# Third node stage of a four-layer graph network: residual and bias summed in PSUM by TensorE instead of in SBUF by VectorE

## The reference

```python
rst = jax.ops.segment_sum(msg, dst, num_segments=N)
rst = rst + bias[None, :, :]
...
x = _layernorm(x + _L2_gnn_ref(x, edge_attr_64, src, dst, ...), axis=-1)
```

## Time and profile before

| | |
|---|---|
| median of three runs | 9195.85 us (9191.78 to 9219.41) |
| profiled execution | 9210.81 us |
| its span | 9209.1 us |
| VectorE busy | 6234.8 us, 68% |
| GpSimd busy | 5451.7 us, 59% |
| TensorE busy | 4799.2 us, 52% |
| ScalarE busy | 3278.4 us, 36% |
| DMA traffic | 1839.84 MB, 200 GB/s |

### The profile page before, as it was taken

One profiled execution on the slowest core, in us unless ns is written; L12 is line 12 of the kernel. 1 busy time (PEld: TensorE's weight loads), 2 busy tenths in 40 slices (PEclk: granted clock), 3 DMA queues, 4 the chain that ended last, 5 costly groups with the idle time before them and its releaser, 6 DMA issues. The chain is left out here.

```text
span 9209.1 us, 103278 instructions
## 1 busy us (share of the span) xinstructions
PE 4799.2 (52%) x18908; PEld 3452.2 (37%) x18908; DVE 6234.8 (68%) x20123; ACT 3278.4 (36%) x8442; POOL 5451.7 (59%) x5121
## 2 busy tenths in 40 slices
PE   8856000039996333347771111100688887899743
PEld 4422000038884211225551111100455555788622
DVE  7899333358887999977777777799544444455566
ACT  4433002347774111126660000144222222344588
POOL 7877777764445666655547777677788888100000
PEclk9999555569997555569995555555777778899855
DMA  0299899989886445459984444588544444566688
GB/s 20 99 344 338 284 309 297 309 274 299 297 294 195 146 146 148 147 173 285 278 268 117 122 122 123 165 266 266 108 79 79 79 79 79 165 200 199 214 292 284
DMA packets 1143019, 1839.84 MB, mean 200 GB/s; under 512 B 218094, under 2 KB 564898, under 8 KB 1142374
## 3 DMA queue, kind: packets, MB, share of 16 engines
q1 hardware_dynamic: 884838, 1245.79, 39.8%
q0 software_dynamic: 257536, 587.44, 26.3%
HBM read 1044.55 MB, written 788.03 MB: 199 GB/s over the span
## 5 line engine op out<-in xcount | busy, mean ns | idle before, releaser
L717 POOL DMA_INDIRECT st<-S,last_i x1176 | 1325.6, 1127 | 897.6 <-DVE yt L759 370.4
L915 POOL DMA_INDIRECT rows<-T,src_i x784 | 800.8, 1021 | 251.1 <-issue 248.1
L642 ACT ACTIVATE xo<-z,shift,rsd 128x256 f32<-128x256 f32 x1568 | 851.0, 591 | 1.3 <-issue 1.1
L1128 POOL DMA_INDIRECT A<-comb,ai x392 | 702.5, 1792 | 159.6 <-issue 145.0
L931 PE MATMUL psE<-encs,attr 4*128 4x256 f32 x784 | 404.9, 668 | 745.2 <-DMA attr<-in_attr3T 745.2
L946 ACT ACTIVATE ex<-diff 128x32 f32<-128x32 f32 x392 | 89.8, 229 | 1709.6 <-DVE diff L993 1709.6
L1200 DVE TENSOR_SCALAR eq<-psI,src_f 128x128 f32<-128x128 f32 x392 | 136.7, 349 | 743.2 <-DMA A<-comb,ai 708.4
L931 PE MATMUL psE<-fes,attr 64*128 64x8 f32 x784 | 199.5, 363 | 821.7 <-DMA attr<-in_attr64T 819.4
L477 DVE SCALAR_TENSOR_TENSOR sums<-sums,same,rows 128x256 f32<-128x256 f32 x784 | 380.2, 485 | 326.6 <-ACT rows L458 312.4
L1142 PE MATMUL psH<-rbf,wf1s 20*128 20x256 f32 x784 | 278.9, 485 | 613.9 <-DMA rbf<-in_rbfT 613.9
L931 PEld LDWEIGHTS psE<-encs,attr 4*128 4x128 f32 x784 | 227.5, 319 | 922.3 <-DMA attr<-in_attr3T 884.7
(11 more groups left out here) (232 smaller groups left out, 15612.8 us busy)
## 6 DMA issues: line engine op xcount, KB each, us to landing
X<-xo SPq DMA_DIRECT2D x588, 256.0 KB
xt<-X SPq DMA_DIRECT2D x588, 256.0 KB
S<-sums SPq DMA_DIRECT2D x392, 272.0 KB, 2.4
A<-zero SPq DMA_DIRECT2D x392, 256.0 KB, 4.8
S<-sums SPq DMA_DIRECT2D x392, 256.0 KB, 4.1
xt<-in_x SPq DMA_DIRECT2D x392, 256.0 KB
T<-tt SPq DMA_DIRECT2D x196, 280.0 KB
T<-tt SPq DMA_DIRECT2D x196, 272.0 KB
```

Source lines behind the costliest of these rows:

```text
L642: ins = e.activation(y[s][:, k, :], z[s][:, k, :], ACT.Identity, bias=shift[s][:, k, :], scale=rsd[s][:, k, :])
L717: e.indirect_dma_start(st[s][:, k, :], None, sums_table, bass.IndirectOffsetOnAxis(ap=last_i[:, c:c + 1], axis=0))\
L915: e.indirect_dma_start(rows[s][:, k, :], None, table, bass.IndirectOffsetOnAxis(ap=src_i[:, c:c + 1], axis=0))\
L1128: e.indirect_dma_start(A[k], bass.IndirectOffsetOnAxis(ap=ai[s][:, k, :], axis=0), comb[s][:, k, :], None, compute_op=ALU.add).then_inc(si ...
```

## The change

`add_bias` is no longer in VectorE's list for `layer` = 2. TensorE gets a part `join_residual` there: for each of the two columns it multiplies the residual by the identity matrix into a PSUM bank and accumulates onto it the product of a row of ones with one row of the bias, so that the bank holds residual plus bias. Two banks `psZ` are used in turn. VectorE's `add` takes its second operand from the bank. A row of 128 ones is set in `setup`.

```diff
+        one_row = sb("one_row", [1, P])
...
+                        e.memset(one_row[:], 1.0)
                         link(e.memset(unit[:], 1.0))
...
-                psZ = [bank(f"psZ{j}", G * D) for j in range(2)] if layer == 0 else None
+                psZ = [bank(f"psZ{j}", G * D) for j in range(2)] if layer != 1 else None
...
                             hold(e, *done(st_["biased"], i, s))
-                            e.tensor_tensor(z[s][:], more, xb[s][:], ALU.add).then_inc(signal(st_["summed"], s), 1)
-
-
-                        unrolled(R, NS, [(combine, 0), (add_bias, 0), (add, ADD), (lambda i, s: ln_invert(e, i, s), APPLY)]
+                            residual = psZ[s % 2][:].rearrange("p (g d) -> p g d", g=G) if layer == 2 else xb[s][:]
+                            e.tensor_tensor(z[s][:], more, residual, ALU.add).then_inc(signal(st_["summed"], s), 1)
+
+
+                        unrolled(R, NS, [(combine, 0)] + ([(add_bias, 0)] if layer < 2 else []) + [(add, ADD), (lambda i, s: ln_invert(e, i, s), APPLY)]
...
+                        def join_residual(i, s):
+                            hold(e, *done(loaded, i, s))
+                            hold(e, *done(st_["summed"], i, s, 2))
+                            for k in range(G):
+                                e.matmul(psZ[s % 2][:, k * D:(k + 1) * D], ident[:], xt[s][:, k, :], start=True, stop=False)
+                                mm = e.matmul(psZ[s % 2][:, k * D:(k + 1) * D], one_row[:], b2s[0:1, :], start=False, stop=True)
+                            mm.then_inc(signal(st_["biased"], s), 1)
+
                         stages = [(turn_r, TURN), (product, PRODUCT)] if layer == 0 else []
+                        stages += [(join_residual, 0)] if layer == 2 else []
```

## The result

The changed kernel takes 9502.57 us (median of 4 runs, 9495.9 to 9509.68) against 9193.82 us of the kernel before (4 runs, 9187.07 to 9219.41). The ratio is 1.0331, 95% interval 1.0309 to 1.0353. It is slower by 308.8 us; the forecast was 9506 us.

What follows compares the result with a forecast made beforehand. The prediction took VectorE and GpSimd, both full at 3.02 us a slot, as the third node stage's bound. TensorE's 4.60 us would replace it: 196 x (4.60 - 3.02) = +310 us on 9195.85, giving 9506 us, range 9268 to 9532.

Steps and rivals of the forecast that it cites:

- What bounded the kernel: Third node stage: VectorE and GpSimd both full at 3.02 us a slot, 196 slots.
- DMA floor: Third node stage: the DMA engines allow no slot below 0.86 x 3.02 = 2.6 us.
- The relief: Third node stage: removing 196 VectorE adds is worth 0 to 0.4 us a slot if nothing new is slower.
- The add from PSUM at nothing: VectorE's remaining add, third node stage: reading its operand from PSUM costs nothing extra (683 against 684 ns elsewhere).
- The products: TensorE, third node stage: four products are 8 instructions a slot, 0.427 us each, 3.42 us bare at 1.2 GHz.
- The alternation: TensorE, third node stage: switching between 128 rows and one makes each group 0.59 + 0.56 us, four groups 4.60 us.
- Rival 4: TensorE, third node stage: the switch costs less, 4.28 us a slot, +247 us, 9443 us; chance 0.12.
- rival 3: TensorE, third node stage: the switch costs nothing for one row, 3.42 us a slot, +78 us, 9274 us; chance 0.07.
- The clock: TensorE, third node stage: the granted clock stays at 0.50 (1.2 GHz), since half the time is one-row products.
- the two stretches with few rows: Earlier TensorE stretches, products of 4 rows and some of 20, full for 5.40 us and 6608.63 to 6615.21, stayed at 1.2 GHz.
- Rival 1: Third node stage: the clock rises to 2.4 GHz, slot near 2.75 us, -53 us, 9143 us; chance 0.09.
- The chain: Third node stage: with two psZ banks TensorE runs without a gap and sets the slot; add, mix and gathers wait.

Runs made afterwards that it cites:

- rows128_act: rows128 with the third node stage's stores of xo issued by ScalarE instead of SyncE; 9101.54 us beside 9199.62 for the kernel before, ratio 0.9894.
- row_only: Changed kernel with the identity product replaced by a one-row product, so every product has one row; 9604.72 us beside 9534.89 for the kernel before, ratio 1.0066.
- rows72: Changed kernel with the bias product padded with zeros to 72 rows; 9160.01 us beside 9186.42 for the kernel before, ratio 0.9966.
- rows128: Changed kernel with the bias product padded with zeros to 128 rows; 9144.78 us beside 9186.42 for the kernel before, ratio 0.9948.
- rows64: Changed kernel with the bias product padded with zeros to 64 rows; 9840.23 us beside 9534.89 for the kernel before, ratio 1.0324.
- before_act: Kernel before with only the third node stage's stores of xo moved to ScalarE; 9558.38 us beside 9567.29 for the kernel before, ratio 0.9991.

## Why the prediction was right

*What bounded the kernel.* I had VectorE and GpSimd both full at 3.02 us, with a DMA floor of 2.6 us. VectorE was. GpSimd was full only because VectorE's operations on two SBUF tiles lengthened its gathers (last section): at the 0.944 us that a gather takes in the changed kernel it needs 2 x (0.944 + 0.30) = 2.49 us a slot. The relief that I put between 0 and 0.4 us is 0.24 to 0.28 us with the queues as they stand (slots of 2.78 and 2.74) and 0.43 in `rows128_act`, whose slot of 2.59 us at a DMA share of 0.96 makes the floor 2.49 and not 2.6. VectorE's own time fell to 416.50 / 174 = 2.39 us a slot, against 2.3. None of this could move the forecast, since TensorE's 4.60 us lie above it all.

*The add from PSUM at nothing.* 686 ns against 684: right.

*The products.* 8 instructions, 0.427 us each: right, bare in `row_only` with one row (0.853 a pair) and in `rows72` with 72 and 128 rows while the clock is low (0.86).

*The alternation.* 0.59 + 0.56 us a pair, for both kinds: right to the hundredth. The two things that no row showed came out on the full side, which was a choice and not a finding: one row behaves as 20, and the 128-row group pays in full behind a change. Rival 4 (4.28 us) and rival 3 (3.42 us) are excluded by the timeline. The rule of the Trainium skill, TensorEngine Tiling (Array Packing), section Key Properties, that a change of tiling mode drains TensorE, agrees with the step between 64 and 72 rows and with the weight loads, of which none runs across a change; that page's list of configurations knows 32, 64 and 128 rows.

*The clock.* 0.50 throughout, as the two stretches with few rows had it. That was thin evidence, 5.40 and 6.58 us long, and behind the first TensorE was busy for only 0.07 of 11.20 us, so that its low clock there says little. That few rows can hold the clock low in a full TensorE was shown only by `row_only`; how much of it the gaps do in the changed kernel is open. Rival 1 was not run: no kernel here has the changes at the high clock. `rows128` has the high clock without them, and its 2.78 us beside my 2.75 come from other floors (TensorE itself is busy for 293.65 of 400 us), which is a coincidence and no support for that sum. The rule that sustained activity releases the throttle (the Trainium skill, TensorE: Matmul & The Clock Gate, Part 1) holds for `rows128` and does not hold for `row_only`, busy for 395 of 400 us at 0.50.

*The sum.* 196 x (4.60 - 3.02) = 310 us against 308.8 measured, and 308 by the two traces' slots.

*The chain.* TensorE without a gap, VectorE waiting for `psZ`, gathers at 0.944 us and waiting for `mix`: as forecast.

What the experiments' expectations missed is the clock with 72 rows, and what the load behind the store was worth.

## What to carry to other kernels

A product of few rows is not a small one. It takes the time of its columns, it costs 0.29 us at the low clock to go to it and again to come back, and where half or all of TensorE's products were such, the clock stayed at 1.2 GHz though TensorE was full. In the filter stage, where 4 instructions of 18 have 20 rows, it does reach 2.4 GHz.

Where a bias is to be added in PSUM, padding its product to all 128 rows (zeros in the weights) turned a loss of 309 us into a gain of 42 to 59, on the chips on which the kernel before takes some 9190 us. On a chip where it takes 9535 us the padded kernel was run only with the later store, and was slower than the kernel before (1.0063).

Two engines that are equally full need not be two limits: here one lengthened the other's instructions. After an engine is relieved, look for the queue in which the next load stands behind a wait; moving that store was worth 35 to 39 us in the padded kernel.

## What the runs showed of the hardware

- The step between 64 and 72 rows: 4.60 us a slot with 1, 32 and 64 rows, 2.90 with 72. The clock went with it, 0.50 and 0.89. Why 72 rows beside 128 let the clock rise and one row in every product doesn't, with no change in either, these runs bound (1 row in every product: 0.50; 72 beside 128: 0.89; 128: 0.97) but don't explain.
- GpSimd's gather got shorter when VectorE had less to do. Its median in the third node stage of the kernel before is 1187 ns; after the change it is 944, in this view of the tile `st` from 5940 to 6740 us of the changed kernel:

```profile
L719 POOL DMA_INDIRECT st<-S,last_i x348: 940/944/961, 5941.3 to 6738.3; - x174
```

- What had lengthened it can be read from the timelines, though no run varied it alone. In the kernel before:

```profile
6103.98 0.69 DVE L766 TENSOR_TENSOR z<-st,den 128x512 f32<-128x512 f32 x1
6104.30 1.19 POOL L717 DMA_INDIRECT st<-S,last_i  x1 [0.30 <-issue]
6105.40 0.69 DVE L779 TENSOR_TENSOR z<-z,xb 128x512 f32<-128x512 f32 x1
6105.80 1.11 POOL L717 DMA_INDIRECT st<-S,last_i  x1 [0.31 <-issue]
```

The first gather is 0.12 us old at 6104.42, when 0.25 us of VectorE's multiplication of two SBUF tiles are left: 0.94 + 0.25 = 1.19. The second is at 6105.92, with 0.17 us of the add left: 0.94 + 0.17 = 1.11. The 0.12 us is fitted. Of the 331 gathers from 5940 to 6440 us, 319 follow this to within 0.02 us. An add with one operand in PSUM doesn't lengthen them; in `rows128`:

```profile
6102.86 0.94 POOL L720 DMA_INDIRECT st<-S,last_i  x1 [1.07 <-DVE z L769]
6102.93 0.69 DVE L783 TENSOR_TENSOR z<-z,psZ 128x512 f32<-128x512 f32 x1 [0.63 <-PE psZ L871]
```

So the change spares GpSimd twice: one add of two SBUF tiles is gone and the other now reads PSUM.

- Chips differ. The kernel before took 9186 to 9200 us on some and 9535 and 9567 on two others. The stage that TensorE set was 4.60 us a slot on both kinds. The same padded kernel with the later store had 2.63 us on one and 3.35 on the other, at DMA shares of 0.94 and 0.75, so that the DMA engines were not full on the slower one; what limits it is open. From 1000 to 1400 us, where TensorE and ScalarE stand idle and VectorE waits for gathers, the traces move 307 GB/s on the faster kind (kernel before) and 274 and 266 on the slower (`rows64`, `before_act`), while the first node stage, 2200 to 2700 us, has 298 on the one and 298 and 296 on the others.
